# A transformer layer on one core: transposes and q, k, v products by halves of the array's rows, and one ring of seven PSUM banks

## What is computed

```python
# attention: 16 heads of 16 channels
qkv = (x @ w_qkv).reshape(b, s, 3, 16, 16)
scores = einsum('bqhd,bkhd->bhqk', q, k) * 16 ** -0.5
out = einsum('bhqk,bkhd->bqhd', softmax(scores), v) @ w_proj + b_proj
x = layernorm(x + out)
# feed-forward: 8 experts, each token goes to its best 2, each expert takes at most 5120
top_v, top_i = top_k(x @ Wg.T, 2)
gates = softmax(top_v)
# expert e: inp, gate = split(rows @ W1[e]);  (gelu(inp) * gate) @ W2[e]
x = layernorm(x + sum over the 2 experts of gates * expert output)
```

## Time and profile before

| | us |
|---|---|
| median of the runs | 3536.07 |
| the profiled execution, its own time | 3539.23 |
| its span | 3537.5 |
| busy: TensorE | 3328.4 (94%) |
| busy: TensorE's weight loads | 2116.9 (60%) |
| busy: VectorE | 2489.7 (70%) |
| busy: ScalarE | 2001.0 (57%) |
| busy: GpSimd | 1156.9 (33%) |

### The profile page before, as it was taken

The page is one execution under the profiler, slowest core; times in us unless marked ns, Lnnn a source line. Parts: engine busy times, 40 slices in busy tenths (PEclk is TensorE's granted clock), DMA queues, the critical chain, the costliest instruction groups (busy, mean ns, idle before and its releaser), DMA issues. The chain is left out here.

```text
span 3537.5 us, 60085 instructions
## 1 busy us (share of the span) xinstructions
PE 3328.4 (94%) x19714; PEld 2116.9 (60%) x19714; DVE 2489.7 (70%) x5865; ACT 2001.0 (57%) x3877; POOL 1156.9 (33%) x925
## 2 busy tenths in 40 slices
PE   6999999999999999999999779999999999999960
PEld 3444444444444444444444368888888888888850
DVE  5888888888888888888888445545554545554439
ACT  2777777777777777777777434444444444444420
POOL 1013232222313131313222243435343435343334
PEclk7999999999999999999999789999999999999985
DMA  3444555333323232333333244444344434442439
GB/s 98 146 152 153 162 157 166 107 96 86 97 79 101 78 100 79 100 83 88 91 83 93 61 80 63 74 65 69 54 72 61 79 61 63 66 62 45 62 68 339
DMA packets 397856, 339.51 MB, mean 96 GB/s; under 512 B 257720, under 2 KB 315456, under 8 KB 397632
## 3 DMA queue, kind: packets, MB, share of 16 engines
q1 hardware_dynamic: 334656, 252.20, 27.3%
q0 software_dynamic: 58368, 67.74, 11.3%
q10 hardware_dynamic: 4608, 16.78, 1.2%
HBM read 89.92 MB, written 152.17 MB: 68 GB/s over the span
## 5 line engine op out<-in xcount | busy, mean ns | idle before, releaser
L882 DVE TENSOR_REDUCE peak<-ps_rows 128x1 f32<-128x512 f32 x2048 | 1340.2, 679 | 284.1 <-PE ps_rows L557 280.2
L648 ACT ACTIVATE probs<-ps_cols 128x512 f32<-128x512 f32 x2048 | 1118.5, 599 | 266.7 <-PE ps_cols L567 254.8
L1091 PE MATMUL ps_hid<-x_hi,stack 128*128 128x512 f32 x2560 | 805.0, 396 | 32.3 <-DVE x_lo L1184 27.8
L567 PE MATMUL ps_cols<-stack 50*128 50x512 f32 x2048 | 797.9, 460 | 6.0 <-ACT probs L648 5.8
L557 PE MATMUL ps_rows<-stack 48*128 48x512 f32 x2048 | 763.4, 450 | 9.9 <-DMA stack<-qk_lo 7.7
L1061 POOL DMA_INDIRECT x<-out,token x320 | 503.8, 1574 | 800.2 <-ACT out L1147 641.4
L1190 DVE TENSOR_TENSOR hid<-ps_hid,act_in 128x512 f32<-128x512 f32 x320 | 218.9, 688 | 597.6 <-ACT act_in L1133 597.3
L1091 PEld LDWEIGHTS ps_hid<-x_hi,stack 128*128 128x128 f32 x2560 | 476.9, 189 | 142.0 <-DVE x_lo L1184 27.9
L580 PE MATMUL ps_pv<-probs,v 128*17 128x512 f32 x4096 | 541.6, 601 | 1.2 <-ACT probs L648 1.2
L557 PEld LDWEIGHTS ps_rows<-stack 48*128 48x128 f32 x2048 | 314.5, 187 | 372.8 <-DVE peak L882 264.5
L1091 PE MATMUL ps_hid<-x_lo,stack 128*128 128x512 f32 x1280 | 505.8, 395 | 0.0
(11 more groups left out here) (131 smaller groups left out, 3603.2 us busy)
## 6 DMA issues: line engine op xcount, KB each, us to landing
stack<-qk_hi SPq DMA_DIRECT2D x1024, 64.0 KB, 2.3
expert_rows<-blank SPq DMA_DIRECT2D x80, 520.0 KB, 3.9
quarters<-expert_rows SPq DMA_DIRECT2D x320, 128.0 KB, 2.7
stack<-qk_lo SPq DMA_DIRECT2D x512, 64.0 KB, 2.3
xs<-in_L_attn_x SPq DMA_DIRECT2D x32, 512.0 KB, 3.7
x<-row SPq DMA_DIRECT2D x32, 512.0 KB
fy<-x SPq DMA_DIRECT2D x32, 512.0 KB, 4.6
out<-fz ACTq DMA_DIRECT2D x32, 512.0 KB, 4.8
```

Source lines behind the costliest of these rows:

```text
L567: pe.matmul(ps_cols[j % 2][:], k_stack[g][part, h, t * P:(t + 1) * P], q_stack[g][part, h, :], start=True, stop=True).then_inc(s_cols, 1)
L648: act.activation(probs[:, j % RING, :], ps_cols[j % 2][:], ACT.Exp, scale=SCALE).then_inc(s_exp, 1)
L882: dve.tensor_reduce(peak[s % 2][:, u:u + 1], ps_rows[n % ROWS][:], AX.X, ALU.max, negate=True).then_inc(s_max, 1)
L1091: last = pe.matmul(ps_hid[f % 2][:, part, :], w[c.par][k][:, cols], xx[c.odd][:, k, :], start=i == 0, stop=i == 3 * KT - 1)
```

## The change

- The iteration is now a table, `ORDER`, of 16 blocks. A block has four pairs (its numbers 0 to 3), one "pv" and the rounds at their places. All engines walk the list `STEPS` made from it.
- The rounds xT, x1T and oT are each one round instead of two. These, qk and v are "halved": each product is made as two, one over array rows 0 to 63 and one over rows 64 to 127, into two banks. For a transpose that means two transposes of 64x128, for q, k and v two partial sums.
- ScalarE copies both banks of a halved round out. GpSimd adds the partial sums of q, k and v, and makes the high and low parts of x, q and k (before: ScalarE and VectorE out of PSUM). Turns are copied to SBUF by ScalarE too, and VectorE works from the copy.
- Seven banks form one ring `ps`, in the order of TensorE's turns (a pair has two turns, a halved round two, another round one); the eighth is pv's. TensorE waits for whoever empties what was in the bank seven turns before (`before`, `wait_bank`).
- GpSimd's order is now: split of x, the four q and k rounds, first half of v, scatters, normalise, second half of v, bias addition.
- Steps of the routing, of the layer norm and the turns have new places.

```diff
+ORDER = [
+    [0, 1, "xT", 2, "pv", 3],
+    [0, "x1T", 1, "pv", "peak3", 2, 3],
+    ["logit", 0, 1, "turn1", 2, 3, "pv"],
+    [0, 1, "qk0", 2, 3, "pv"],
+    [0, 1, "qk1", 2, 3, "logitT", "pv"],
+    [0, 1, "peak0", 2, 3, "pv"],
+    [0, 1, 2, "pv", "turn2", 3],
+    [0, "qk2", 1, 2, 3, "pv"],
+    [0, 1, "qk3", 2, 3, "pv"],
+    [0, 1, "v0", 2, 3, "pv"],
+    [0, "place", "peak1", 1, 2, "turn3", 3, "pv"],
+    [0, 1, "oT", 2, "pv", 3],
+    [0, 1, "proj0", 2, "pv", 3],
+    [0, 1, "proj1", 2, 3, "pv"],
+    ["peak2", 0, "turn0", 1, 2, 3, "pv"],
+    [0, 1, "v1", 2, 3, "pv"],
+]
...
+HALVED = ("xT", "x1T", "oT", "qk", "v")
+BANKS = 7
...
+    def bank(self, turn):
+        return (self.b * len(TURNS) + PLACE[turn]) % BANKS
...
-        ps_rows = [psum(f"ps_rows{i}", [P, SEQ]) for i in range(ROWS)]
-        ps_cols = [psum(f"ps_cols{i}", [P, SEQ]) for i in range(2)]
+        ps = [psum(f"ps{i}", [P, SEQ]) for i in range(BANKS)]
         ps_pv = psum("ps_pv", [P, SEQ])
-        ps_round = [psum(f"ps_round{i}", [P, SEQ]) for i in range(2)]
...
@@ sync: reload of a stack
-                        wait_emptied(sp, s_free, it.emptied("qk3", off - 1))
+                        sp.wait_ge(s_lo, (b + off) * 4 + 4)
...
@@ gpsimd, new ahead of the scatters
+                def add_values(n):
+                    wait_emptied(pool, s_free, it.emptied(f"v{n}"))
+                    values = v[(it.odd + 1) % 2][:, 2 * n:2 * n + 2, :, 0:HD]
+                    pool.tensor_tensor(values, values, v_part[:].rearrange("p (t h d) -> p t h d", t=2, h=HEADS),
+                                       ALU.add).then_inc(s_v, 1)
+                if it.on(1):
+                    for n in range(KT):
+                        wait_emptied(pool, s_free, it.emptied("xT"))
+                        pool.tensor_copy(x_t_hi[:, n, :], x_t[:, n, :]).then_inc(s_xhi, 1)
+                        pool.wait_ge(s_xhi, (b + 1) * KT + (n + 1))
+                        pool.tensor_tensor(x_t_lo[:, n, :], x_t[:, n, :], x_t_hi[:, n, :].bitcast(F32),
+                                           ALU.subtract).then_inc(s_xlo, 1)
+                    for n in range(4):
+                        wait_emptied(pool, s_free, it.emptied(f"qk{n}"))
+                        pool.tensor_tensor(qk[n % 2][:, 0], qk[n % 2][:, 0], qk[n % 2][:, 1], ALU.add).then_inc(s_qk, 1)
...
+                        pool.tensor_copy(qk_hi[par][:, n, :], qk[n % 2][:, 0]).then_inc(s_hi, 1)
...
+                        pool.tensor_tensor(qk_lo[par][:, n, :], qk[n % 2][:, 0], qk_hi[par][:, n, :].bitcast(F32),
+                                           ALU.subtract).then_inc(s_lo, 1)
...
@@ tensor
+                def turn_halves(tiles):
+                    for i, tile in enumerate(tiles):
+                        for a, bank in enumerate(banks):
+                            part = slice(a * HALF, (a + 1) * HALF)
+                            last = pe.transpose(bank[0:tile.shape[1], i * HALF:(i + 1) * HALF], tile[part],
+                                                ident[part, part])
+                    return last
...
                 elif kind == "qk":
                     if n == 0:
-                        result_of("xT1")
+                        pe.wait_ge(s_xlo, (b + 1) * KT + KT)
                     for k in range(KT):
                         for p, (w, tok) in enumerate([(w_qk_hi, x_t_hi), (w_qk_hi, x_t_lo), (w_qk_lo, x_t_hi)]):
-                            last = pe.matmul(ps_m[:], w[:, k, n, :], tok[:, k, :], start=k + p == 0,
-                                             stop=(k, p) == (KT - 1, 2))
+                            for a, bank in enumerate(banks):
+                                part = slice(a * HALF, (a + 1) * HALF)
+                                last = pe.matmul(bank[:], w[part, k, n, :], tok[part, k, :], start=k + p == 0,
+                                                 stop=(k, p) == (KT - 1, 2))
...
@@ scalar, empty(name)
+                    elif kind == "qk":
+                        for a in range(2):
+                            copy_out(qk[n % 2][:, a], banks[a][:])
+                    elif kind == "v":
+                        copy_out(v[(it.odd + 1) % 2][:, 2 * n:2 * n + 2, :, 0:HD],
+                                 banks[0][:].rearrange("p (t h d) -> p t h d", t=2, h=HEADS))
+                        copy_out(v_part[:], banks[1][:])
+                    elif kind == "turn":
+                        copy_out(pv_t[:], banks[0][:])
...
@@ vector: low_part, low_x gone
```

More of the change, by code:

```diff
@@ new lines @@
+STEPS = []
+for c_, order_ in enumerate(ORDER):
+    for step_ in order_:
+        if isinstance(step_, int):
+            STEPS.append(("pair", c_ // TILES, HG * (c_ % TILES) + step_))
+        else:
+            STEPS.append(("values" if step_ == "pv" else "round", c_, step_))
+NAMES = [step_[2] for step_ in STEPS if step_[0] == "round"]
+OFFSETS = {"xT": 1, "qk": 1, "v": 1, "turn": -1, "oT": -1, "proj": -1, "peak": 0,
+           "x1T": -2, "logit": -2, "logitT": -2, "place": -2}
+OFFSET = {n: OFFSETS[n.rstrip("0123")] for n in NAMES}
@@ new lines, with pieces_of @@
+OFFSET["turn0"], OFFSET["peak3"] = 0, -1
+HALVED = ("xT", "x1T", "oT", "qk", "v")
+BY_DVE_KINDS = ("proj", "place", "logitT")
+def pieces_of(name):
+    return [(name, i) for i in range(2 if name.rstrip("0123") in HALVED else 1)]
+PIECES = [piece_ for n_ in NAMES for piece_ in pieces_of(n_)]
+BY_DVE = [piece_ for piece_ in PIECES if piece_[0].rstrip("0123") in BY_DVE_KINDS]
+BY_ACT = [piece_ for piece_ in PIECES if piece_ not in BY_DVE]
+BANKS = 7
+TURNS = []
+for kind_, where_, which_ in STEPS:
+    if kind_ == "pair":
+        TURNS += [("rows", where_ * UNITS + which_), ("cols", where_ * UNITS + which_)]
+    elif kind_ == "round":
+        TURNS += [("round", piece_) for piece_ in pieces_of(which_)]
@@ L70, in rows_unit, with cols_of @@
+PLACE = {turn: i for i, turn in enumerate(TURNS)}
+def cols_of(s):
+    return (s + 2) % 4, -1 if s < 2 else 0
 def rows_unit(j):
@@ L84, in settle, with wait_emptied @@
     engine.sem_inc(sem, 1)
-def wait_emptied(engine, s_free, bank_and_value):
-    bank, value = bank_and_value
-    wait(engine, s_free[bank], value)
+def wait_emptied(engine, s_free, by_and_value):
+    by, value = by_and_value
+    wait(engine, s_free[by], value)
 class Iteration:
@@ L144, in iterations, with before @@
-def iterations(engine, n_seq, body, fills=2):
+    def bank(self, turn):
+        return (self.b * len(TURNS) + PLACE[turn]) % BANKS
+    def before(self, turn):
+        i, ago = PLACE[turn] - BANKS, 0
+        while True:
+            if i < 0:
+                i, ago = i + len(TURNS), ago + 1
+            kind, which = TURNS[i]
+            if self.b - ago < -1:
+                return "none", 0, 0
+            off = 0 if kind == "rows" else OFFSET[which[0]] if kind == "round" else cols_of(which // UNITS)[1]
+            if self.on(off - ago):
+                return kind, which, ago
+            i -= BANKS
@@ L147, in iterations @@
+def iterations(engine, n_seq, body, fills=4):
     for b in range(-1, n_seq + 2):
@@ L242, in attention @@
         pv = sb("pv", [P, SEQ])
+        pv_t = sb("pv_t", [P, SEQ])
         rsum = sb("rsum", [P, UNITS])
@@ L587, in _ @@
+                for kind, where, which in STEPS:
+                    if kind == "pair":
+                        pair(where, which)
+                    elif kind == "values":
+                        values(where)
+                    elif it.on(OFFSET[which]):
+                        round_(it, which)
             iterations(pe, n_seq, body)
```

483 lines of the change are left out of this document (236 added, 247 removed).

## The result

Against a forecast of 2.8% the change gave 1.1%: 3492.35 us (median, 3491.9 to 3494.8) against 3532.8 us for the kernel before on the same chip, ratio 0.989, 95% interval 0.9875 to 0.9906. The time lies inside the range that I gave (3385 to 3525 us), but less than half of the forecast gain is there. The profiled execution took 3492.51 us, its span 3490.8.

A forecast was written before the change was run, and what follows sets the result against it. TensorE, full in the steady attention stage, was taken as the bound: 60.41 - 3.1 - 0.7 + 0.2 = 56.8 us a sequence; 108 + 2 - 12 = 98 us saved, giving 3438 us, 2.8% faster; range 3385 to 3525 us.

The forecast's parts named there:

- halved transposes: Transposes of x, x1 and o: six rounds become three of eight half steps at 0.13 us, saving 0.42 us a sequence.
- halved products: q, k, v rounds on 64 rows, two halves side by side: saves 0.72 us (q, k) and 0.40 (v) a sequence.
- I put 0.2 us for it: TensorE's wait at qk0 for GpSimd's 24.4 us chain, which just fits: 0.2 us a sequence, bounds 0 and 4.
- Rival (2): GpSimd's chain decides: operations a tenth slower, TensorE loses 2 us at qk0 each iteration; 3492 us, chance 0.14.
- VectorE's 47.7 us: VectorE's work a sequence: 4.1 of 51.8 us moves away (low parts of q, k, x); expected near 48.
- The ring: Seven banks walked in TensorE's order shorten waits of rows and cols: 0.7 us a sequence, bounds 0 and 2.0.
- rival (4): The ring gives its upper bound, 2.0 us: 55.3 us a sequence, 3393 us, chance 0.08.
- TensorE's slots: Steps of 0.23 to 0.24 us in qk, 0.12 in v, 0.13 in transposes, with no gap at their edges.
- Rivals (1): Halves don't run side by side, their weight loads take turns: 62.0 us a sequence, 3594 us, chance 0.11.
- (3): Halved rounds still pay both edges, as another shape; only the ring's gain remains: 9 us, 3527 us, chance 0.05.
- 62 ns: Sequencer cost per matmul: a v round of 1.49 us, not 1.38; 2.9 us a sequence saved, time 6 us more.
- Once per launch: Before the first rows GpSimd's split is uncovered: 12 us later, bounds 8 and 16; first rows at about 55 us.

The follow-up runs named there:

- ladder: Six kernels on chip A, us a sequence: before 60.43, full_both 58.95, full_products_3 58.04, the change 58.51, fp_adds 59.85 (59.68 used), ring_off_3 63.34.
- full_products_3: The change with q, k, v products on all 128 rows, no GpSimd additions for them, one ScalarE copy, transposes still halved; 3473.79 us, ratio 0.985 on A.
- fp_adds: full_products_3 with GpSimd's six additions a sequence kept, of zeros; 3529.09 us, ratio 1.000 on A.
- idle_adds: The kernel of full_products_3 with six unneeded additions a sequence in GpSimd's idle time, off its chain; 3744.84 us, ratio 0.996 on B, against 0.977 without them.
- fp_late: full_products_3 with the scatters moved one iteration later, behind the split of x; 3556.92 us, ratio 1.007 on A.
- ring_off_3: The change with its seven banks split 3/2/2 again (rows, cols, rounds) instead of one ring; 3641.69 us, ratio 1.032 on A; 1.017 on B, twice.
- full_both: The change with no halves: transposes and products on all 128 rows; ring, table and GpSimd's split remain; 3501.38 us, ratio 0.992 on A.
- pool_load: The kernel before with 28 unneeded 128x512 additions a sequence on GpSimd; 3878.12 us, ratio 1.031 on B.
- late_scatter: The change with the scatters moved one iteration later, behind the split of x; 3709.99 us, ratio 0.985 on B.

## Why the prediction was wrong

By its own terms the forecast of -3.6 us a sequence splits into the rungs of the ladder. The new table has 33 stretches of pairs without any half, 30 with halved transposes, 24 with all.

| rung | forecast, us | measured |
|---|---|---|
| ring, split, table (edge +0.19, ring -0.7, GpSimd +0.2) | -0.3 | -1.5 |
| halved transposes (-0.42, 3 edges -0.57) | -1.0 | -0.9 |
| halved products (-1.12, 6 edges -1.14) | -2.3 | +0.5 |
| sum | -3.6 | -1.9 |

- **The failed step: "I put 0.2 us for it", GpSimd's chain as the whole price of its work, with VectorE's durations left as they were.** Of the -2.3 us for halved products nothing is left. The additions that they need cost 1.6 us a sequence beside products on all rows (58.04 to 59.68, full_products_3 to fp_adds), within my bound of 4 but mostly for another reason: off the chain the same additions cost as much (idle_adds), because GpSimd's instructions hold VectorE's. Halving the products gives 1.2 back (59.68 to 58.51), ScalarE's copies included, half of what I had: net +0.5. Inside the change the two can't be told apart so well: fp_adds has VectorE at 52.6 us, with peak_parts held, the change at 50.8, with row_count held instead, so the additions may cost less there, and the halves bring less, than these two steps say.
- **The chain itself was mis-sized too.** TensorE's own waits for it are 1.0 us a sequence (x1's rows 0.7, the low part of x 0.3), not 0.2. Rival (2) had the time nearest to the result, 3492, by luck: its mechanism is a part of it, but qk0 waits 0.3 us for the low part of x, not 2, and GpSimd's operations are not slower than their rows.
- **VectorE's 47.7 us were 50.8.** I subtracted 4.1 us of moved work and took the rest at its old durations. By their lengths, counts grew by 3 x (0.42 - 0.16) = 0.8 us, row_count by 0.8, o by 4 x (0.52 - 0.41) [0.41 in the kernel before, out of PSUM] = 0.4; the casts of peak_parts shrank by 4 x (0.29 - 0.17) = 0.5. That is 1.5 of the 3.1 us. The rest isn't a matter of longer instructions: VectorE's records overlap at their ends and busy time counts an overlap once, so it fell by less than the 4.1 us of length that went. How held operations become waits of TensorE is seen in the 0.41 us ahead of qk3, in idle_adds and in fp_late; its wait of 0.2 us ahead of v1 is released by a reduction of VectorE too.
- **The ring was mis-sized.** I took 0.7 us of a bound of 2.0; it carries 4.8 in this kernel (58.51 to 63.34), more than rival (4) had. Against it stands the split on GpSimd with the table, some 2.1 us slower on B. Together they did better than forecast, -1.5 instead of -0.3. How much of the 2.1 us is table and how much GpSimd was not taken apart. The bound was drawn from the waits for cols and rows in the old order; in the new table without the ring the cols' wait on TensorE itself is 1.9 us alone (ring_off_3), and where the other 2.9 us lie was not taken apart.
- **TensorE's slots were right.** No edges, 0.23 and 0.115 us. The transposes were better, 0.46 us for each of the three rounds instead of 8 x 0.13 = 1.04, 1.7 us a sequence more than I had. I had put their step between 0.115 and 0.148 us, by the columns of weights; the rows say 64x64, so 64 columns pass in each instead of the 128 of the earlier trace rows, and two halves step by 0.058 us. The ladder shows none of it, the rung gave 0.9: in full_both TensorE is busy in 1293.75 of 1300 us, in full_products_3 in 1284.57, so part of what its slots gave became waits. Rivals (1) and (3) are out. The prediction weighed the 62 ns that the Trainium skill (page TensorE: Matmul & The Clock Gate, section "Wait — 56ns, not 53.3ns?") gives for each matmul without hardware decoding. That price isn't paid here: 24 products of v in 12 x 0.115 us are 58 ns each, and 0.46 / 16 is 29 ns. Which way matmuls are decoded no run here shows.
- **Once per launch.** The first rows of pairs come at 49.23 us, 6.1 later instead of 12; in full_both and full_products_3 they come at 44.50 and 44.12, so most of the 6.1 comes with the halved products. It is less than 12 because GpSimd's cast takes 0.61 us, not 0.78, and VectorE's 16 casts of weights take 3.83 us instead of 8.18, because GpSimd's two additions to x (2.3 us each), beside which two of the casts took 2.34 and 2.37 us before, now come later.
- **Three long iterations**, 9 us, which I had not foreseen: in two of them the first scatter is followed by a gap of 4 us on GpSimd. Before, it was hidden (gaps of 3.7 to 4.0 us are in that trace, three times); now it stands in the chain, and x1's rows are 4 us late. What makes the gap stays open:

```profile
1028.36 1.12 POOL L504 DMA_INDIRECT expert_rows<-row,slot  x1 [8.61 <-DVE token L954]
1033.45 0.99 POOL L504 DMA_INDIRECT expert_rows<-row,slot  x1 [3.96 <-issue]
```

Sum: 30 x 1.9 = 57, less 9, less 6, is 42 us; measured were 40.

## What to carry to other kernels

Work moved to GpSimd isn't free because GpSimd is idle: price it also by what VectorE does from SBUF meanwhile. Here an addition of 1.28 us cost 0.2 to 0.3 us, on the chain or off it, and 0.14 in pool_load; in fp_late a mere change of order cost 83 us, as another addition came to lie beside a subtraction of VectorE. So look at which VectorE operations it falls beside, and what waits behind them. Halving the array's work pays where its results need no extra operation; here the transposes paid and the products did not. And a bound on a change of buffers that is drawn from the waits of the old order need not hold in a new one.

## What the runs showed of the hardware

**A small VectorE operation with both inputs in SBUF can last until GpSimd's instructions beside it end.** Sixteen columns took 2.89 us beside an addition of 2.37 us and the cast behind it (fp_late), eight columns 0.95 us beside an addition of 1.28 (the change); the shortest of either kind take 0.16 us. VectorE's reductions out of PSUM kept their mean of 0.68 us, with GpSimd's load and without.

**A pause costs twice.** In a long iteration TensorE waits 4.15 us for x1's rows, and its granted clock drops (windows of the change, columns as in the earlier trace rows):

```profile
1040.00:1044.00 4.00, 4.00 (x42) 1.63 (x42) 3.34 (x7) 4.00 (x9) 3.34 (x5) 1.00 0.55 173
1044.00:1048.00 4.00, 0.60 (x4) 0.18 (x4) 1.29 (x2) 1.84 (x4) 4.00 (x4) 0.85 0.39 99
1048.00:1052.00 4.00, 3.25 (x26) 1.33 (x26) 0.69 (x1) 1.57 (x3) 4.00 (x3) 0.50 0.14 33
1052.00:1056.00 4.00, 4.00 (x29) 1.77 (x25) 2.54 (x5) 2.77 (x7) 3.73 (x5) 0.80 0.10 33
```

0.50 is the lower level, 1.2 GHz; from 1056 us on the clock is 1.00 again.

**Chips differ by 6% on the same program.** On A and on the chip of the result the kernel before took 3527 to 3537 us in every run, on the three chips called B 3751 to 3768. On those, VectorE and ScalarE stop together for some 4 us about once a sequence, and around it TensorE's granted clock is at the lower level for mostly 7 to 10 us. VectorE and then ScalarE in late_scatter on B:

```profile
1249.95 0.69 DVE L978 TENSOR_REDUCE peak<-ps 128x1 f32<-128x512 f32 x1 [3.85 <-remote]
```

```profile
1249.97 1.07 ACT L704 COPY qk<-ps 128x512 f32<-128x512 f32 x2 [4.01 <-remote]
```

It is in all variants there, and what causes it stays open. It changes what a kernel's parts are worth: ring_off is 1.032 on A and 1.017 on B.
